# Key projection in three single-pass products of split parts, with new slot tables and ScalarE copies, in a decoder layer on one core

## What is computed

```python
q = (query @ Wq + bq)          # 16 heads of 8
k = (key_value @ Wk + bk)      # key_value: 32 x 1500 x 96
v = (key_value @ Wv + bv)
attn = jnp.einsum('bhqd,bhkd->bhqk', q, k) * scale
attn = jax.nn.softmax(attn, axis=-1)
x = jnp.einsum('bhqk,bhkd->bqhd', attn, v).reshape(B, Nq, Cq)
return x @ Wo + bo
```

## Time and profile before

| | |
|---|---|
| median of 3 runs | 936.07 us (934.58 to 936.29) |
| profiled execution, its own time | 932.99 us |
| its span | 931.2 us |
| TensorE busy | 890.5 us, 96% of the span |
| VectorE, ScalarE, GpSimd busy | 718.7, 628.9, 366.0 us |
| chain that ended last | TensorE 91%, VectorE 4%, ScalarE 2% |

### The profile page before, as it was taken

The page is one execution under the profiler, slowest core; times in us unless marked ns, Lnnn a source line. Parts: engine busy times, 40 slices in busy tenths (PEclk is TensorE's granted clock), DMA queues, the critical chain, the costliest instruction groups (busy, mean ns, idle before and its releaser), DMA issues.

```text
span 931.2 us, 25904 instructions
## 1 busy us (share of the span) xinstructions
PE 890.5 (96%) x10439; PEld 732.4 (79%) x10439; DVE 718.7 (77%) x1481; ACT 628.9 (68%) x1081; POOL 366.0 (39%) x351
## 2 busy tenths in 40 slices
PE   5789999999999999999999999999999899999995
PEld 4657888887888888787888888878787788999894
DVE  6677787777777777777777777777777767777996
ACT  3666777777777777777777777777775644445554
POOL 6553443333333333333333333333354432114992
PEclk9999999999999999999999999999999999999998
DMA  6549666765556666666555667666546000002321
GB/s 148 114 115 210 143 144 140 151 144 126 126 126 138 148 148 146 139 145 140 126 125 127 143 141 157 144 146 146 127 100 146 25 23 24 23 24 105 138 101 43
DMA packets 36530, 112.37 MB, mean 121 GB/s; under 512 B 8322, under 2 KB 18884, under 8 KB 36292
## 3 DMA queue, kind: packets, MB, share of 16 engines
q1 hardware_dynamic: 36404, 110.64, 52.4%
HBM read 32.23 MB, written 1.89 MB: 37 GB/s over the span
## 4 chain that ended last, share of the span: by engine, by line
PE 91%; DVE 4%; ACT 2%; issue 1%; DMA 0%; SPq 0%; POOL 0%; ACTq 0%; DVEq 0%
PE psum L1443 19%; PE psum L1628 18%; PE psum L1689 13%; PE psum L1450 9%; PE psum L1455 8%; PE psum L1693 4%; PE psum L1716 3%; PE psum L1729 3%; PE psum L1717 3%; PE psum L1718 3%; PE psum L1728 3%; PE psum L1730 3%; DVE arena L962 1%; DVE arena L901 1%; PE psum L1761 0%
## 5 line engine op out<-in xcount | busy, mean ns | idle before, releaser
L962 DVE TENSOR_REDUCE arena<-psum 128x1 f32<-128x500 f32 x672 | 435.7, 674 | 151.2 <-PE psum L1443 146.3
L773 ACT ACTIVATE arena<-psum 125x896 f32<-125x896 f32 x384 | 334.5, 915 | 119.0 <-PE psum L1628 61.3
L1443 PE MATMUL psum<-K_hi,Q_bd 128*128 128x500 f32 x672 | 285.7, 464 | 6.2 <-DVE arena L962 2.9
L547 POOL TENSOR_TENSOR arena<-arena,K_hi 128x500 fp32r<-128x500 f32 x96 | 119.9, 1249 | 375.9 <-ACT K_hi L705 375.9
L1628 PEld LDWEIGHTS psum<-Q_st,K_st 103*125 103x125 f32 x1536 | 210.4, 189 | 15.6 <-issue 2.3
L1628 PE MATMUL psum<-Q_st,K_st 103*125 103x224 f32 x1536 | 215.3, 274 | 2.0 <-DVE Q_st L977 1.3
L1443 PEld LDWEIGHTS psum<-K_hi,Q_bd 128*128 128x128 f32 x672 | 123.1, 190 | 57.0 <-DVE arena L962 31.2
L1689 PE MATMUL psum<-arena 125*25 125x168 f32 x3072 | 157.8, 308 | 0.3 <-issue 0.2
L829 ACT ACTIVATE K_st<-psum 128x448 fp32r<-128x448 f32 x128 | 69.7, 544 | 79.3 <-PE psum L1718 77.8
L1693 PE MATMUL psum<-arena 125*9 125x56 f32 x3072 | 108.8, 213 | 0.3 <-issue 0.3
L1450 PEld LDWEIGHTS psum<-WvA,arena 97*125 97x125 f32 x768 | 100.4, 190 | 3.9
(11 more groups left out here) (258 smaller groups left out, 1021.5 us busy)
## 6 DMA issues: line engine op xcount, KB each, us to landing
K_st<-K_hi SPq DMA_DIRECT2D x256, 187.5 KB, 4.9
K_st<-arena SPq DMA_DIRECT2D x128, 187.5 KB, 3.4
arena<-in_ctx SPq DMA_DIRECT2D x32, 562.5 KB, 7.1
arena<-gate_rows SPq DMA_DIRECT2D x8, 896.0 KB, 4.3
arena<-in_L_ffn_W SPq DMA_DIRECT2D x16, 256.0 KB, 3.1
arena<-OS_all SPq DMA_DIRECT2D x12, 168.0 KB, 6.9
x_rows<-x_all SPq DMA_DIRECT2D x1, 896.0 KB, 10.1
out<-x_all SPq DMA_DIRECT2D x4, 224.0 KB, 3.0
```

Of the source, the lines that this page charges most:

```text
L547: g.tensor_tensor(low.bitcast(F32R), low, K_hi[:, par, n * KB:n * KB + KB].bitcast(F32), ALU.subtract).then_inc(F["keys_low"], 1)
L773: a.activation(P2[c % NP].rearrange("p (n k) -> p n k", n=2), psum[0:CK, 2 + 2 * (c % 2):4 + 2 * (c % 2), 0:HQ // 2], ACT.Exp)\
L962: v.reduce_max(mx[:, par, n // NB, n % NB:n % NB + 1], bank_of(n)[:, 0:KB], AX.X).then_inc(F["piece_max_taken"], 1)
L1443: mm(bank_of(n)[:, 0:KB], Q_bd[:, par].rearrange("p h q -> p (h q)")[:, 128 * (n // NB):128 * (n // NB) + 128], K_hi[:, par, (n % NB) * KB ...
```

## The change

Four things change. (1) The key projection of batches 2 to 31 is made of float32r parts: GpSimd splits each block of the context (`split_context`, two instructions on 97x500) and once the weights into high and low, and TensorE makes three single-pass products high·high, high·low, low·high into one bank. `ctx_split` holds one block alone, so the split of block `n` waits for the product of block `n-1`. (2) The tables place K, V, P, O and VectorE's small steps anew; the outputs stand in four runs (slots 2, 6, 9, 11) where there were three (5, 7, 11). (3) GpSimd's period is reordered, with the low keys of block 2 before those of block 1. (4) In periods 30 and 31 ScalarE makes the copies of `projected` and `normed` of quads 0 to 2 that VectorE made. To make room, early weights and masks move into the place of the fourth `P2` buffer.

```diff
-V_SLOTS = (9, 11, 1)
-K_SLOTS = (3, 5, 7)
-COPY_SLOT, SUM_SLOTS, SCALE_SLOT = 0, (0, 3, 3, 3), 5
+V_SLOTS = (9, 11, 3)
+K_SLOTS = (1, 5, 7)
+COPY_SLOT, SUM_SLOTS, SCALE_SLOT = 0, (2, 3, 5, 5), 6
...
-OUTPUTS = {5: ((0, 0), (0, 1), (0, 2), (0, 3)), 7: ((0, 4), (0, 5), (0, 6), (0, 7)), 11: ((0, 8), (0, 9), (0, 10), (0, 11))}
+OUTPUTS = {2: ((0, 0), (0, 1)), 6: ((0, 2), (0, 3), (0, 4), (0, 5)), 9: ((0, 6), (0, 7)), 11: ((0, 8), (0, 9), (0, 10), (0, 11))}
...
+            def split_context(b, par, n, load):
+
+                if load:
+                    pool.wait_ge(D_[f"c{par}"], 16 * load)
+                pool.wait_ge(F["keys_made"], b * NB + n + PRIME)
+                part = ctxT2[:, par, n * KB:n * KB + KB]
+                high, low = ctx_split[0:DC + 1, 0], ctx_split[0:DC + 1, 1]
+                step(g.tensor_tensor(high, part, ones[0:DC + 1, 0:1].to_broadcast([DC + 1, KB]), ALU.mult))
+                g.tensor_tensor(low, part, high.bitcast(F32), ALU.subtract).then_inc(F["context_split"], 1)
...
             def period(b, par, half):
                 if has(b, 2):
-                    pool.wait_ge(F["max_scores_made"], (b + 1) * PIECES + PRIME)
-                    spread_queries(b + 2, par)
+                    split_context(b + 2, par, 1, 0)
                 if has(b, 1):
...
                     stack_queries(b + 1, 1 - par)
                 if has(b, 2):
-                    low_keys(b + 2, par)
+                    pool.wait_ge(F["max_scores_made"], (b + 1) * PIECES + PRIME)
+                    spread_queries(b + 2, par)
+                if has(b, 2):
+                    split_context(b + 2, par, 2, 0)
+                if has(b, 2):
+                    low_keys(b + 2, par, (0,))
+                if has(b, 2):
+                    low_keys(b + 2, par, (2,))
+                if has(b, 2):
+                    low_keys(b + 2, par, (1,))
+                if has(b, 3):
+                    split_context(b + 3, 1 - par, 0, half + 2 + par)
                 if isinstance(b, int) and b == 1:
                     later_constants()
...
+                    P = passes[0]
+                    if isinstance(b, int) and b == B - 2:
+                        if c == 5:
+                            projected(P, 0)
+                        if c == 8:
+                            projected(P, 1)
+                    if isinstance(b, int) and b == B - 1:
+                        if c == 0:
+                            normed(P, 0)
+                        if c == 1:
+                            projected(P, 2)
+                        if c == 4:
+                            normed(P, 1)
             periods(act, period)
...
+            def key_project_split(b, par, n):
+
+                pe.wait_ge(F["context_split"], b * NB + (n + 1) + PRIME)
+                for i, (w, x) in enumerate(((0, 0), (0, 1), (1, 0))):
+                    last = mm(bank[7][:, 0:KB], Wk_split[:, w], ctx_split[0:DC + 1, x], start=(i == 0), stop=(i == 2))
+                last.then_inc(F["keys_made"], 1)
```

More of the change, by code:

```diff
@@ L116, in decoder_kernel @@
         perm = sb("perm", [128, SLOTS, 128])
-        w_sb = {n: sb(n + "_sb", [128, 128]) for n in ("wq", "wk", "wv", "xWq", "xWo")}
-        qk = sb("qk", [128, 128])
+        ctx_split = sb("ctx_split", [128, 2, KB], F32R)
+        Wk_split = sb("Wk_split", [DC + 1, 2, 128], F32R)
+        xWo_sb = sb("xWo_sb", [128, 128])
         bq_col = sb("bq_col", [128, 1])
@@ L160, in decoder_kernel @@
         start = used[0]
+        first_place = whole[:, start + NP * HQ - HQ:start + NP * HQ]
+        w_sb = {n: first_place[:, 128 * i:128 * i + 128] for i, n in enumerate(("wq", "wk", "wv", "xWq"))}
+        w_sb["xWo"] = xWo_sb[:]
+        qk = first_place[:, 512:640]
+        other_batch, causal = [first_place[0:TT, 640 + TT * i:640 + TT * i + TT] for i in range(2)]
         def first_buffers(place):
@@ L580, in _ @@
             low_queries(3)
+            pool.wait_ge(D_["keyw"], 16 * 2)
+            step(g.tensor_tensor(Wk_split[:, 0], WkA[:], ones[0:DC + 1], ALU.mult))
+            step(g.tensor_tensor(Wk_split[:, 1], WkA[:], Wk_split[:, 0].bitcast(F32), ALU.subtract))
+            pool.wait_ge(S1["queries_made"], NQ)
+            split_context(2, 0, 0, 2)
             def period(b, par, half):
                 if has(b, 2):
-                    pool.wait_ge(F["max_scores_made"], (b + 1) * PIECES + PRIME)
-                    spread_queries(b + 2, par)
+                    split_context(b + 2, par, 1, 0)
                 if has(b, 1):
@@ L1385, in first_values @@
                 for t in range(QT):
-                    last = mm(bank[4 + n % 2][0:TT, D * t:D * t + D], firsts[n].xT[:, TT * t:TT * t + TT], w_sb["wv"][:], start=True, stop=True)
+                    last = mm(bank[4 + n % 2][0:TT, D * t:D * t + D], firsts[n].xT[:, TT * t:TT * t + TT], w_sb["wv"], start=True, stop=True)
                 last.then_inc(S1["values_made"], 1)
@@ L1482, in _ @@
             pe.wait_ge(weights, 16 * 3)
-            mm(bank[0][:, 0:128], w_sb["wq"][:], w_sb["wk"][:], start=True, stop=True).then_inc(w_ps, 1)
+            mm(bank[0][:, 0:128], w_sb["wq"], w_sb["wk"], start=True, stop=True).then_inc(w_ps, 1)
             pe.wait_ge(w_ev, 1)
@@ L1637, in period @@
                             project(P, 0)
[L1638 removed]
+                        if c == 6:
                             turned(P, 0)
```

88 lines of the change are left out of this document (36 added, 52 removed).

## The result

The changed kernel took 925.78 us (median of 5 runs, 921.91 to 927.17) against 935.69 us (5 runs, 934.58 to 936.29) of the kernel before: a ratio of 0.9898, 95% interval 0.9883 to 0.9913, or 9.9 us less. The forecast was 5.1 less, at 931.0. The direction was right and both medians lie in the range, but the gain is 1.9 times the forecast in the first pair and 1.5 times in the second.

The account below looks back on a forecast made before the run. TensorE's own work was taken to bound the steady periods. Terms -7.8, -0.3, +5.4 and -2.4 made -5.1 us: 927.9 against the profiled 932.99, so a median of 931.0; 8 in 10 within 924 to 937.

Parts of the forecast that it names:

- period 0: First period, bound by 28 reductions: the new tables were to save 0.3 us.
- periods 1 to 29: Steady periods: 0.14 us from cheaper key products less a fourth output run, plus 0.13 from waits; 20.8 each, -7.8 in all.
- constants: Period 2: splits queue behind GpSimd's one-time constants; 3.7 and 1.4 us late, 0.3 for low clock, +5.4 in sum.
- tail (P30, P31, rest): Periods 30, 31 and after: copies moved to ScalarE save 1.6, 1.1 and 0.3 us, two output runs add 0.66; -2.4.
- the last addition: Whole kernel: 3.1 us, the old kernel's median above its profiled execution, added to 927.9 to give a median of 931.0.
- K at P's price: Key projection on TensorE: three products at 0.228 us, a piece's price, make 0.68 against 0.84, saving 0.47 a period.
- 0.33 of a fourth run: TensorE's outputs: one more run's begin and end cost 0.33 us a period, without cover.
- K1's lateness: Period 2: the split of block 1 waits behind GpSimd's constants, so TensorE's second key product starts 3.7 us late.
- constants without cost: Rival, chance 0.2: GpSimd catches up or other waits in period 2 hide the lateness; +5.4 falls away, 925.5 us.
- No handoff bit: Rival, chance 0.2: five handoffs with 0.05 us to spare run 0.1 longer, costing 0.25 a period; 938 us.
- Splits late in every period: Rival, chance 0.1: block 2's split exceeds 3.25 us and K2, its key product, waits each period; 941.5 us at 3.6.
- K at 0.21: Rival, chance 0.05: the key projection's products take nearer 0.21 us each on TensorE; 4 us less, 927.

Follow-up runs that it names:

- a_again: The changed kernel as it is, profiled and timed again: 926.23 us, ratio 0.9909 to the kernel before; its profiled execution took 926.64 us.
- a_fp32: The changed kernel with each key product one float32 product again and no GpSimd splits: 933.62 us, ratio 0.9991 to the kernel before.
- a_oldtables: The changed kernel with all tables of the kernel before: 1015.0 to 1017.3 us in three of four runs, ratio 1.0865 to the kernel before.
- a_threeruns: The changed kernel with outputs in three runs of four (slots 5, 7, 11) instead of four runs: 985.51 us, ratio 1.0554 to the kernel before.
- a_dvecopies: The changed kernel with the copies of quads 0 to 2 back on VectorE: 926.21 us, ratio 0.9912 to the kernel before.

## Why the prediction was right and wrong

Here are its terms beside what a_again, the usual execution of the changed kernel by its time, shows against the kernel before, from the table:

```
term                       forecast   measured
start                         0        +1.0   (first profile: -3.5)
period 0                     -0.3      -1.5
periods 1 to 29              -7.8     -10.6   (constants taken out)
constants                    +5.4      +6.8   (27.57 - 20.72)
tail (P30, P31, rest)        -2.4      -1.9
sum                          -5.1      -6.2
```

**The step that failed most** is none of the kernel's terms but the last addition: "Its median stands 3.1 above that, at 936.07, so the median becomes 931.0." It took the distance from profiled execution to median, found in three runs of the kernel before, as the same for both kernels. The runs showed otherwise. The kernel before stands 2.7 above its profiled execution in its five runs and 1.4 above its two profiled executions over 46; the changed kernel's a_again, at 926.64, stands 0.4 above its own median of 926.23 and 0.9 above the first one. What fills the distance is in the main low clock that the profiled executions of the kernel before didn't have (0.991 and 0.989 granted, against 0.984 to 0.987 in its slower runs); where in the kernel it lies stays open. Of the 4.8 us by which the measured gain (9.9) exceeds the forecast (5.1), 2.7 are this offset, 0.9 lie between a_again and the first median, and 1.2 are the terms.

**The sum of the terms** was only 1.3 off (927.9 against 926.64), and in part by luck: their errors are -2.8 in the periods, -1.2 in period 0, +1.4 in the constants, +1.0 in the start and +0.5 in the tail.

**Periods.** K at P's price was right: 0.68, and 0.47 a period by a_fp32. So was the 0.33 of a fourth run (0.32). What was mis-sized is "I take 0.27 a period", where a usual period lost 0.33: the tables took 0.14 where 0.33 less 0.13 make 0.20, and the stray delays of before (0.6 in period 1, another 0.6 in periods 4 to 27) are gone too, where I subtracted from their mean and kept them. That is 2.8 over 29 periods, the largest error in a term. In period 0 I gave the tables 0.3; without the splits it was 1.0 shorter, and with them 0.5 more.

**Constants.** K1's lateness was forecast at 3.7 and is 3.61, by the mechanism named. The 1.4 at K2 isn't there, and the 0.3 for the clock is 2.9: the clock was already low when K1's first product came, and stretched the way from K1 to K2 from 4.35 to 7.26, so that K2's split came in time and there was no second wait to hide it in. Two errors of opposite sign, -1.4 and +2.6, that cancel in part: the term was 1.4 too small by a_again, and 1.3 by the first profiled execution. The rival "constants without cost" fell.

**Start.** It stood in no term. In a_again that is 1.0 too little; in the first profiled execution it was wrong by 3.5, by a race that stood in the profile of before, a step of 4.90 us on four columns, which I didn't follow up. It tells that two profiled executions of one kernel can differ by 4.5 us.

**Tail.** The wait of 1.65 at quad 1's transposes is gone, as forecast, and period 30 with its fourth run is 1.8 shorter. Behind period 31 I took 1.1 off the wait of 1.19, and it is still 0.81: 0.4 of the 1.1 came. Low clock in the expert stage, which stood in no term, took up to 1.7 back, and period 31 is 0.5 shorter where I gave it a run more. The whole tail was 0.5 short of the forecast. (The four numbers of its sum make -2.3, not -2.4.)

**Rivals.** No handoff bit: from 300 to 700 us TensorE is busy 399.97 of 400, and by the prediction's prices the work of a period is 20.75 less 0.47 and more by 0.33, 20.61, where it measures 20.72. Splits late in every period is real in a_oldtables only. K at 0.21 fell with 0.68 for three. The side (faster by over 0.2%) was right.

## What to carry to other kernels

A gain per period is best measured by taking a single part back (here 0.47 for the split, 0.14 against it for the tables), and a one-time job on an engine that has become part of the chain belongs in pieces into its idle time: 10.5 us of constants cost 6.8 in one place and at most 0.9 in two. With the fill of K_st in four as well the kernel takes 915.0 us, 2.1% less than before and 11 us less than the changed one. Less work on the bound engine can be slower (a_threeruns), when the work removed was what let another engine run ahead. And a forecast for a median should be made from several profiled executions: add the profile's difference to the median only as far as the offset is known for both kernels, and look at the granted clock of each run first.

## What the runs showed of the hardware

- A GpSimd fill of 5.09 us, which writes 7 partitions and reads nothing, holds a VectorE TENSOR_SCALAR of 0.17 us in SBUF for 4.90 us. A TENSOR_TENSOR, a SCALAR_TENSOR_TENSOR and a TENSOR_REDUCE that ran beside such a fill of 5.13 took their usual 0.62 (the changed kernel's first profiled execution).
- Which step the fill holds can change from one execution of a kernel to the next: 59.33 against 63.86 us for the first scores of the changed kernel, from a step that begins 0.08 ahead of the fill or 0.71 behind it.
- Whether a wait of 1.9 us is followed by low clock isn't set by the wait's length alone: after it the granted clock was 0.75 over 6.8 us in the changed kernel's first profiled execution and 1.00 in a_dvecopies.
- At the end of TensorE's 3.6 us without work the granted clock fell to 0.50; TensorE then worked 6.2 us at 0.51, which cost 2.9 us, nearly as much as the wait.
